# Three result tables in place of four in a graph kernel's scatter stage

## What is computed

```python
es = ys[dst]; ev = yv[dst]
m0a = wA * es * sh0
m0b = wD * jnp.einsum('eud,ed->eu', ev, sh1) * INV_SQRT3
m1a = wB[:, :, None] * es[:, :, None] * sh1[:, None, :]
m1b = wC[:, :, None] * ev * sh0[:, :, None]
ns = jax.ops.segment_sum(concat(m0a, m0b), src, N)      # and nv from m1a, m1b
deg = jax.ops.segment_sum(ones, src, N)
dn = jax.lax.rsqrt(jnp.maximum(deg, 1.0))
os_ = (ns * dn[:, None]) @ w2_s * inv2 + sc_s           # and ov from nv
...                                                     # rms norms, then
x = layernorm(x + concat(os_, ov))
```

## Time and profile before

| | us |
|---|---|
| median of 3 runs | 6196.12 (6193.98 to 6201.93) |
| the profiled execution, its time | 6189.36 |
| its span, first to last instruction | 6187.6 |

### The profile page before, as it was taken

The page is one execution under the profiler, slowest core; times in us unless marked ns, Lnnn a source line. Parts: engine busy times, 40 slices in busy tenths (PEclk is TensorE's granted clock), DMA queues, the critical chain, the costliest instruction groups (busy, mean ns, idle before and its releaser), DMA issues.

```text
span 6187.6 us, 209904 instructions
## 1 busy us (share of the span) xinstructions
PE 5737.5 (93%) x40694; PEld 4573.5 (74%) x40695; DVE 5531.1 (89%) x17615; ACT 3280.7 (53%) x11999; POOL 4743.6 (77%) x4057
## 2 busy tenths in 40 slices
PE   6899999999999997889999999999999999999966
PEld 5555555555555554559999999999999999999944
DVE  2899999999999988989999999999999999999978
ACT  2566666666666654545555555555555555555522
POOL 2777777777777764548888888888888888888878
PEclk8999999999999998889999999999999999999999
DMA  6799999999999984459999999999999999999998
GB/s 198 222 264 263 263 263 263 263 263 264 264 264 263 264 253 152 157 147 178 178 178 178 175 177 176 176 175 175 177 174 177 175 176 174 177 176 174 167 298 294
DMA packets 1269400, 1298.01 MB, mean 210 GB/s; under 512 B 220911, under 2 KB 1180656, under 8 KB 1269264
## 3 DMA queue, kind: packets, MB, share of 16 engines
q0 software_dynamic: 328176, 468.28, 46.3%
q1 hardware_dynamic: 941186, 829.31, 45.6%
HBM read 695.20 MB, written 601.74 MB: 210 GB/s over the span
## 4 chain that ended last, share of the span: by engine, by line
PE 30%; DMA 14%; issue 9%; POOL 5%; DVE 2%; POOLq 1%; ACT 0%; SPq 0%; DVEq 0%; ACTq 0%
DMA part<-arena,c_idx 14%; PE PS L964 8%; PE PS L946 7%; PE PS L935 5%; PE PS L979 5%; PE PS L962 4%; POOL part L584 1%; POOL arena L565 1%; POOL arena L561 1%; POOL d_n L602 1%; POOL out L596 0%; PE PS L954 0%; DVE arena L1302 0%; ACT arena L753 0%; DVE arena L1299 0%
## 5 line engine op out<-in xcount | busy, mean ns | idle before, releaser
L584 POOL DMA_INDIRECT part<-arena,c_idx x1664 | 2615.1, 1572 | 538.3 <-issue 349.3
L545 POOL DMA_INDIRECT big<-h_tab,big x1664 | 1631.4, 980 | 511.7 <-issue 385.6
L860 PE MATMUL PS<-big 128*128 128x260 f32 x3328 | 953.2, 409 | 162.5 <-DVE big L1154 158.2
L964 PE MATMUL PS<-w2m,arena 128*128 128x128 f32 x6656 | 1103.8, 288 | 0.0
L946 PE MATMUL PS<-arena 128*128 128x256 f32 x3328 | 863.1, 382 | 27.9 <-ACT arena L753 26.7
L1162 DVE TENSOR_TENSOR big<-big,PS 128x260 f32 x1664 | 703.2, 423 | 207.9 <-PE PS L860 150.7
L964 PEld LDWEIGHTS PS<-w2m,arena 128*128 128x128 f32 x6656 | 876.9, 192 | 0.0
L860 PEld LDWEIGHTS PS<-big 128*128 128x128 f32 x3328 | 563.7, 189 | 422.6 <-issue 343.9
L659 ACT ACTIVATE big<-PS,arena 128x128 f32<-128x128 f32 x1664 | 513.6, 359 | 667.1 <-PE PS L850 667.1
L752 ACT COPY arena<-PS 128x512 f32<-128x512 f32 x832 | 488.7, 587 | 524.1 <-DMA part<-arena,c_idx 469.0
L729 ACT COPY arena<-PS 128x384 f32<-128x384 f32 x1664 | 718.6, 486 | 31.0 <-PE PS L935 2.8
(11 more groups left out here) (180 smaller groups left out, 10924.2 us busy)
## 6 DMA issues: line engine op xcount, KB each, us to landing
w_tab<-big SPq DMA_DIRECT2D x416, 520.0 KB
arena<-w_tab SPq DMA_DIRECT2D x1664, 130.0 KB
part<-arena SPq DMA_DIRECT2D x1664, 32.1 KB
ot_tab<-big SPq DMA_DIRECT2D x416, 128.0 KB
arena<-ot_tab SPq DMA_DIRECT2D x416, 128.0 KB
arena<-src_tab SPq DMA_DIRECT2D x416, 128.0 KB
arena<-part SPq DMA_DIRECT2D x392, 128.5 KB, 3.5
big<-h_tab,big POOLq DMA_INDIRECT x1664
```

The source lines that it names most:

```text
L545: pool.indirect_dma_start(hg[:, s, k, :], None, h_tab, bass.IndirectOffsetOnAxis(ap=sidx[:, s, k:k + 1], axis=0)).then_inc(s_hg[s], 16)
L584: pool.indirect_dma_start(part[q], bass.IndirectOffsetOnAxis(ap=c_idx[:, s, k:k + 1], axis=0), o_cmb[:, s, k, :], None, compute_op=ALU.add ...
L860: mm(PS[:, 2 + k % 2, 0:HW], oh[:, p, k, :], hg[:, p, k, :], start=True, stop=True).then_inc(s_agg, 1)
L964: last = mm(o_v[:, k, 2 * j:2 * j + 2, :].rearrange("p j u -> p (j u)"), midT[:, k, 1 + j, :], w2m[:, (1 + 2 * j) * MUL:(3 + 2 * j) * MUL] ...
```

## The change

Three tables take the place of four (`PARTS` = 3). Tile t goes to table `part[t % 3]`, so its scatter waits for that of tile t - 3. Landings are counted in eight semaphores, one for each of the two tiles of a pair and each of the four staging slots, in place of one a table. GpSimd's loop body has twelve pairs in place of four, since tables repeat after three tiles, tiles of a pair after two and slots after four pairs. Stage A zeroes three tables, stage D loads and adds three.

```diff
@@ -45,6 +45,7 @@
 TURN = 4
+PARTS = 3
 
@@ -114,7 +115,7 @@
     ZERO = -(-(NP + P) // (NG * 32))
-    part = [dram(f"part{k}", [NG * 32 * ZERO, OR], F32) for k in range(GROUP)]
+    part = [dram(f"part{k}", [NG * 32 * ZERO, OR], F32) for k in range(PARTS)]
 
@@ -276,7 +277,7 @@
 
-        d_p = cut(TURN * GROUP * OR, True).rearrange("p (s k d) -> p s k d", s=TURN, k=GROUP)
+        d_p = cut(TURN * PARTS * OR, True).rearrange("p (s k d) -> p s k d", s=TURN, k=PARTS)
         d_x = cut(TURN * 2 * D).rearrange("p (s d) -> p s d", s=TURN)
@@ -303,7 +304,8 @@
             "c", "y sh same ix pr mid cnt num mt mT o os ov turn sum cmb")
-        s_cw, s_add = sems("c_w", slots), sems("c_add", slots)
+        s_cw = sems("c_w", slots)
+        s_add = [sems(f"c_add{k}", slots) for k in range(PAIR)]
         s_cin, s_cpa = sems("c_in", "0 1"), sems("c_pa", "0 1")
@@ -400,7 +402,7 @@
                 if there(g):
-                    for k in range(GROUP):
+                    for k in range(PARTS):
                         sp.dma_start(part[k][ds(g * (32 * ZERO), 32 * ZERO), :].rearrange("(p r) d -> p (r d)", p=32),
@@ -422,7 +424,7 @@
             sp.wait_ge(s_acc, GROUP * NG)
-            sp.wait_ge(s_zero, 16 * GROUP * NG)
+            sp.wait_ge(s_zero, 16 * PARTS * NG)
             xb = x.rearrange("(b p) d -> b p d", p=P)
@@ -471,14 +473,15 @@
 
-            for k in range(GROUP):
-                sp.wait_ge(s_add[k], 16 * NG)
+            for s in range(TURN):
+                for k in range(PAIR):
+                    sp.wait_ge(s_add[k][s], 16 * (NU // TURN))
             pb = [q[0:NP, :].rearrange("(b p) d -> b p d", p=P) for q in part]
 
             def step_d(b, s, there):
                 if there(b + 4):
                     wait(sp, s_dsum, b + 1)
-                    for k in range(GROUP):
+                    for k in range(PARTS):
                         sp.dma_start(d_p[:, s, k, :], one(pb[k], b + 4)).then_inc(s_din[s], 16)
@@ -571,20 +574,31 @@
 
-            pool.wait_ge(s_zero, 16 * GROUP * NG)
+            pool.wait_ge(s_zero, 16 * PARTS * NG)
             pool.wait_ge(s_w, 16 * N_W)
 
-            def step_c(u, s, there):
-                if there(u):
-                    wait_apart(pool, s_cix, 2 * (u + 1))
-                    for k in range(PAIR):
-                        q = s % 2 * PAIR + k
-                        wait_apart(pool, s_ccmb, u + 1)
-                        wait_apart(pool, s_add[q], 8 * u - 8 * (s % 2))
-                        pool.indirect_dma_start(part[q], bass.IndirectOffsetOnAxis(ap=c_idx[:, s, k:k + 1], axis=0),
-                                                o_cmb[:, s, k, :], None, compute_op=ALU.add).then_inc(s_add[q], 16)
-
-            steps(pool, NU, 0, 0, step_c)
+            ROUND = PARTS * TURN
+
+            def step_c(u, j, rounds):
+                wait_apart(pool, s_cix, 2 * (u + 1))
+                for k in range(PAIR):
+                    t = j * PAIR + k
+                    before = t - PARTS
+                    wait_apart(pool, s_ccmb, u + 1)
+                    wait_apart(pool, s_add[before % PAIR][before // PAIR % TURN],
+                               rounds * (16 * PARTS) + 16 * (before // (PAIR * TURN) + 1))
+                    pool.indirect_dma_start(part[t % PARTS],
+                                            bass.IndirectOffsetOnAxis(ap=c_idx[:, j % TURN, k:k + 1], axis=0),
+                                            o_cmb[:, j % TURN, k, :], None, compute_op=ALU.add
+                                            ).then_inc(s_add[k][j % TURN], 16)
+
+            for j in range(ROUND):
+                step_c(j, j, 0)
+            with pool.Fori(1, NU // ROUND) as i:
+                for j in range(ROUND):
+                    step_c(i * ROUND + j, j, i)
+            for j in range(NU % ROUND):
+                step_c(NU // ROUND * ROUND + j, j, NU // ROUND)
 
@@ -742,13 +756,12 @@
                 if there(u - 3):
-                    q = o % 2 * PAIR
                     wait(act, s_ccnt, u - 2)
                     wait(act, s_cix, 2 * (u - 6))
                     a.copy(c_num[:, o, :, :], counts).then_inc(s_cnum, 1)
                     wait_apart(act, s_cnum, u - 2)
                     for k in range(PAIR):
-                        wait(act, s_add[q + k], 8 * (u - 3) - 8 * (o % 2) - 16 if there(u - 7) else 0)
+                        wait(act, s_add[k][o], landed(u - 7, o) if there(u - 7) else 0)
                     a.copy(o_cmb[:, o, :, 0:D], summed)
@@ -994,10 +1007,10 @@
                 if there(b + 3):
-                    wait(pe, s_din[n], landed(b + 3, n, GROUP))
+                    wait(pe, s_din[n], landed(b + 3, n, PARTS))
                     wait(pe, s_do, b)
-                    for k in range(GROUP):
-                        last = mm(PS[:, n, 0:OR], ident[:, :], d_p[:, n, k, :], start=(k == 0), stop=(k == GROUP - 1))
+                    for k in range(PARTS):
+                        last = mm(PS[:, n, 0:OR], ident[:, :], d_p[:, n, k, :], start=(k == 0), stop=(k == PARTS - 1))
                     last.then_inc(s_dsum, 1)
@@ -1325,7 +1338,7 @@
                     for k in range(PAIR):
-                        wait(dve, s_add[m % 2 * PAIR + k], 8 * (u - 8) + 16 - 8 * (m % 2) if there(u - 8) else 0)
+                        wait(dve, s_add[k][m], landed(u - 8, m) if there(u - 8) else 0)
                     v.tensor_tensor(c_idx[:, m, :], c_d[:, m, :], srcF[:, ds((u - 4) * PAIR, PAIR)], ALU.max
```

## The result

The changed kernel takes 6496.53 us (median of 4 runs, 6488.46 to 6504.96) against 6195.05 us (6187.7 to 6201.93): a ratio of 1.0491, 95% interval 1.0476 to 1.0505. It is slower by 301 us. The profiled execution took 6488.46 us, its span is 6486.7 us.

The account below looks back on a forecast made before the run. GpSimd's scatter pace was taken to bound stage C. Span 6187.6 us, +266 for waits, -4 for stage D, 1.8 around it, and 6.8 from profiled run to median gave 6458 us; range 6290 to 6590.

Parts of the forecast that it names:

- What bounds the kernel: Stage C goes at GpSimd's pace, 1.88 us a scatter; TensorE is 0.06 us a pair behind; GpSimd's losses count in full.
- The price of a wait: Stage C: a held scatter starts 0.75 us after the landing it waits for; three tables hold latencies over 4.89 us.
- The walk over nine latencies: Stage C: start conditions applied in order to nine latencies of the earlier trace; pace settles at 2.06 us a scatter, +300 us.
- the feedback: Stage C: a slower pace thins SP's loads and the overlap of scatters, taking 0.1 to 0.2 us off the latency.
- Loop of twelve pairs: GpSimd's loop: fewer loop edges save up to 24 us or a longer body costs as much; taken as 0.
- Counting by slot: Completion counted per staging slot: as many waits for ScalarE and VectorE, 0; SP's four more waits under 0.3 us.
- stage A: 1248 zeroing stores instead of 1664, off the path: 0, at most 51 us if GpSimd's pace were not the bound.
- Stage D, -4 us: Three loads and products a block gain 2 us; four fewer load issues at its start gain 1.9 us.
- A hidden wait (1, 2): Stage C's pace stays 1.88 us: 6168 to 6192 us with loop-edge gains (5%), 6184 to 6208 without (4%).
- Full cost (3): Stage C: latencies cost in full without feedback, 2.16 us a scatter, 6658 us, or near 6550 for a mixture; 20%.
- The clock (4): Stage C: TensorE idles more and its clock falls to 0.87, a pair takes 4.25 us, 6600 us; 6%.
- the +83 us: Stage C: lower bound on the waits' cost from the mean latency, 1.93 us a scatter instead of 1.88.

Follow-up runs that it names:

- the light loads with four tables: The kernel before, with SP loading only the first 128 of 260 columns of each w_tab row inside the loop: 6161.24 us, ratio 0.995.

## Why the prediction was right, and where it was off

- **What bounds the kernel.** Right. 302 us lost at GpSimd's pace in stage C were 301 us lost in all. Of the experiments only the light loads with four tables had TensorE as the bound.
- **The price of a wait, 0.75 us from landing to start.** Right to the hundredth, with two and three tables and with four tables and a wait of three.
- **The walk over nine latencies.** It gave 2.06 us a scatter with nothing taken off, and 2.06 was measured; I had forecast 2.04 for the feedback. That agreement is luck, as misses balance in it. The feedback was larger than allowed: the mean latency fell by 0.31 us, not 0.1 to 0.2. The walk with 0.31 us less each settles at 1.99, about +180 us, while the waits cost more: idle beyond the plain 0.305 us came to 239.3 us, before 4.6, so +235 against the forecast +266. Nine latencies are too few to give this sum closely.
- **The mean scatter taken as constant.** This is the term that was missing. I carried 1.57 us over from the earlier trace rows. The waits put the first scatter of every second pair where the compare starts: 242 scatters over 1.7 us instead of 81, 241 of them such first ones, and +68 us in all. 235 + 68 = 303. Breaking up the compare took 79 us off the scatters and added 20 us of idle; the median fell by 53.
- **Loop of twelve pairs, +-24 us.** Zero was right; the long scatters did not go with the loop edges (84 of them with a third of the edges, before 81), and 70 of the 81 had started while a compare ran.
- **Counting by slot, stage A.** Zero each, as taken. The 51 us that the stores might have been worth in stage A did not come: the gathers' pace stayed.
- **Stage D, -4 us.** -3 by the profiles.
- **Rivals.** A hidden wait (1, 2) would have needed latencies under about 4.1 us; they were 4.77. Full cost (3) was not reached either. The clock (4) stayed at 1.00 in stage C with TensorE busy 465 of 500 us; with two tables it was lower, without a slower pace where it was.
- **The signs.** Idle of 774.7 us (some 800), the pair at 4.12 us (4.08) and stages A and D came as said. TensorE's busy share was 0.93, not 0.91. One sign did not come: "most idle times no longer 0.30". 1212 of 1664 scatters still started after at most 0.33 us of idle; the 451 held ones brought the added idle, 0.53 us each on average. Nor does the profile put the idle down to the landing of `part`; that took starts and landings side by side.
- **The range.** It was given two high ends, 6540 and 6590; 6496.53 lies under both. Its low end, 6290, does not follow from the +83 us, which give 6196 - 4 + 83 = 6275.

The median came out 38.5 us over the 6458 that I gave, some 37 us more in stage C than my 266 (303) and 1 us less in stage D.

## What to carry to other kernels

A wait that never holds anything may have little slack: set its distance in steps against the latency plus the time from a landing to the start it releases, and do it for the distribution, since an engine with no spare time never catches up on the late ones. Going from a round of 7.52 us to one of 5.64, with 5.1 us of latency and 0.75 to restart, cost 4.9% here; saving a quarter of the tables' loads gave back 3 us. A new wait also shifts its engine against the others, and can place it where a shared resource is taken, so the durations of before are not a given.

## What the runs showed of the hardware

- A GpSimd DMA that was held started 0.75 us after the landing it waited for, in 415 of 440 cases with three tables and 1220 of 1258 with two, while unheld ones follow each other after 0.305 us. Why a restart costs more than that is not shown.
- A scatter that starts during VectorE's 128x512 compare of two SBUF tensors lasts longer by what is left of the compare, less 0.13 us, in 249 of 281 cases: up to 2.07 us instead of 1.55. Sums and products with both operands in SBUF do the same (76 of 87), those with an operand in PSUM do not (1 of 251).
- The latency of a scatter moves with the pace: 5.08 us on average at 1.88 us a scatter, 4.77 at 2.06, 4.47 at 2.67.
